# A transformer block on one Trainium2 core: output additions moved at the change of batches, and the last tiles of the down projection begun early

## The chip, the cores and the metric

The kernel runs on one core of a Trainium2 chip. The metric is the device time in microseconds (us) of one execution; lower is better. Engines are named as in the profile: PE is TensorE, DVE VectorE, ACT ScalarE, POOL GpSimd, SP SyncE, which issues all the DMAs here.

## What is computed

```python
mod = (_silu(c) @ wmod).reshape(4, 6, 1, -1)
sa, ca, ga, sb, cb, gb = (mod[:, i] for i in range(6))
...
h = _layernorm(x) * (1 + ca) + sa
x = x + ga * gated_delta_attention(h)
h = _layernorm(x) * (1 + cb) + sb
x = x + gb * ((silu(h @ w_gate.T) * (h @ w_up.T)) @ w_down.T)
```

`x` is (4, 512, 512) in float32, the hidden size of the last line is 2048. The change touches that last line alone, the feed-forward part.

## The kernel before

The first half of the program does the attention part and stores its result `x` to `scrX`. From about 520 us on the feed-forward part runs as 16 iterations (`iteration(it)`, L1011). Iterations 0 to 7 do the batches 0 and 1, iterations 8 to 15 the batches 2 and 3; each iteration does 256 of the 2048 hidden units for 1024 tokens. Every step is written once into a plan (`step(...)`), and each engine goes through the plan and takes the steps that concern it. So the order of the steps in the plan is the order on each engine, and what an engine waits for is written as semaphores.

One iteration has these steps.

- Two products of seven parts, for gate (`n = 2 * it`) and up (`n = 2 * it + 1`): `prod(n, 0..6)` on PE, six matmuls each. Float32 numbers are split into a high and a low part. ACT copies (`copy_s`, three of them for each `n`) and DVE additions (`cadd`) combine the parts; `prod` 2, 4 and 5 wait for one such copy each.
- The weights of the next product: loaded by SP (`w_load`), combined by four operations of POOL (`w_comb`, L2683 to L2689), high part by ACT (`w_high`), low part by seven operations of POOL (`w_low_ff`, L2696). The down weights have ACT and then four POOL operations (`w_high_d`, L2704). `prod(n, 0)` waits for the low part.
- `silu` (ACT), `gated` (DVE), the rounding of the result (`fh`, ACT) and its low part (`fl`, DVE).
- `down(it, k)` for eight tiles `k` of 128 tokens: six matmuls into one of the banks 6 and 7 in turn, then DVE adds the bank to the row `YA[k]` (iterations 0 and 8 copy). PE may write a bank again once DVE has read it. `down(it - 1, k)` stands among the products of iteration `it`.

At the end of iteration 7's sums DVE multiplies each row `YA[k]` by the gate (`post_0`); in iteration 8 POOL adds the stored `x` (`add_0`, L2732, 512 columns, eight operations), and SP stores the eight rows (`store_0`). `down` of iteration 8 writes `YA[k]` anew in iteration 9.

In the last iteration POOL prepares each row with two operations of 512 columns (`out_pre`, L2739 and L2742): `YA[k]` by the gate `gbB`, then plus `XO[k]`, which is the stored `x`. `down(15, k)` then needs two DVE operations: the bank by the gate, and plus `YA[k]` (L2565 on). `XO[0]` to `XO[5]` are loaded in iteration 10; `XO[6]` and `XO[7]` lie where the gate weights are and are loaded in iteration 15:

```python
if 6 in st["ks"]:
    e.wait_ge(sem("prod"), 7 * 30 + 7)
    e.wait_ge(*at_least(w_low_at[45]))
...
for k in st["ks"]:
    e.dma_start(XO[k][:, :], scrX[2 + k // 4, k % 4 * 128:k % 4 * 128 + 128, :]).then_inc(
        sem(f"d_x{2 + k // 4}"), 16)
```

The second operation of `out_pre` waits for `e.wait_ge(sem(f"d_x{2 + k // 4}"), 80 + 64)`. Before these loads the semaphore stands at 80, and each row adds 16, so for `k` from 4 to 7 it takes the rows 4, 5, 6 and 7.

Of the kernel before, what the change touches and what calls it, by code (L numbers as in the profile page):

```python
# [53 lines left out]
def build(nc, x, W1, cw, dtb, alog, nw, Wo, cT, wmod, wgu, wdn, cst, out):  # L54
# [840 lines left out]
    def down(it, k):  # L895
        i, free = ring_bank()
        step("down", it=it, k=k, bank=i, free=free)
        tick("down")
        ring_free[i] = [tick("v_y")]
        if it == 7:  # L900
            step("post_0", k=k)
        if it == 14:
            step("out_pre", k=k)

# [106 lines left out]
    def iteration(it):  # L1011
# [36 lines left out]
        elif it:  # L1048
            prod(n, 0)
            prod(n, 1)  # L1050
            copy_s(n, 0)
            flush()
            prod(n, 2)
            cadd(n, 0)
            prod(n, 3)
            copy_s(n, 1)
            if last:
                w_high(up_m(it), [("prod", 7 * (n - 1) + 7)])
            step("silu", it=it, t=0)
            prod(n, 4)  # L1060
            copy_s(n, 2)
            cadd(n, 1)
            down(it - 1, 0)
            if not last:
                w_high(up_m(it), [("prod", 7 * (n - 1) + 7)])
            step("silu", it=it, t=1)
            w_load_next(it, w_low_ff(up_m(it)))
            prod(n, 5)
            prod(n, 6)
            step("silu", it=it, t=2)  # L1070
            cadd(n, 2)
            step("silu", it=it, t=3)
        if not last:
            w_comb(gate_m(it + 1))
        for k in range(1, 7):
            if it and (it < 15 or k < 4):
                down(it - 1, k)
            if it in (1, 2) and k in (1, 2, 3, 4):
                turn_tile(4 * it - 4 + k - 1)
                if it == 1:  # L1080
                    step("load_xf", n=k + 3)
# [41 lines left out]
        cadd(n, 1)  # L1123
        if it and not last:
            down(it - 1, 7)
        if turn:
            split_h(1, 4, [("prod", 7 * n + 5)])
            w_high_d(7)
        else:
            gated(it, 1)  # L1130
            w_high_d(it)
            if it == 8:
                for k in range(8):
                    step("add_0", k=k)
            fh(it, 1)
# [130 lines left out]
    def sync(e):  # L1266
# [21 lines left out]
        for st in plan:  # L1288
# [152 lines left out]
            elif kind == "store_0":  # L1441
                k = st["k"]
                e.wait_ge(sem("p_out"), k + 1)
                e.dma_start(out[k // 4, k % 4 * 128:k % 4 * 128 + 128, :], X1[k][:, :]).then_inc(sem("d_out"), 16)
            elif kind == "load_xo":
# [9 lines left out]
            elif kind == "down" and st["it"] == 15:  # L1455
                k = st["k"]
# [5 lines left out]
    def tensor(e):  # L1462
# [11 lines left out]
        for st in plan:  # L1474
# [370 lines left out]
            elif kind == "down":  # L1845
# [9 lines left out]
                for jj, t_ in enumerate(((0, 2), (3, 1))[b]):  # L1855
                    f = f_of(it, t_)
                    t = mm3(bank(st["bank"]), FH[f][:, tk], FL[f][:, tk], WDh[it // 15][:, jj, :], WDl[it // 15][:, jj, :], jj == 0, jj == 1)
                t.then_inc(sem("down"), 1)

# [318 lines left out]
    def vector(e):  # L2178
# [16 lines left out]
        for st in plan:  # L2195
# [357 lines left out]
            elif kind == "down":  # L2553
# [3 lines left out]
                if it % 8 == 0:  # L2557
                    if it:
                        e.wait_ge(sem("p_out"), k + 1)
# [4 lines left out]
                elif it < 15:  # L2564
                    e.wait_ge(sem("v_y"), 8 * (it - 1) + k + 1)  # L2565
                    tt(y, bank(st["bank"]), y, ALU.add).then_inc(sem("v_y"), 1)
                else:
                    e.wait_ge(sem("p_out"), 8 + 2 * k + 2)
                    tt(XO[k][:, :], bank(st["bank"]), gbB[k // 4][:, :], ALU.mult).then_inc(sem("v_y"), 1)
                    e.wait_ge(sem("v_y"), 8 * it + k + 1)  # L2570
                    tt(y, y, XO[k][:, :], ALU.add).then_inc(sem("out_x"), 1)
            elif kind == "post_0":
# [6 lines left out]
    def gpsimd(e):  # L2579
# [11 lines left out]
        for st in plan:  # L2591
# [125 lines left out]
            elif kind == "split_h" and st["on"] == "p":  # L2717
# [8 lines left out]
                signal(t, "p_hs")  # L2726
            elif kind == "add_0":
                k = st["k"]
                e.wait_ge(sem("v_om"), k + 1)
                e.wait_ge(sem(f"d_x{k % 2}"), (160, 144)[k % 2])  # L2730
                in_order()
                signal(e.tensor_tensor(X1[k][:, :], YA[k][:, :], X1[k][:, :], ALU.add), "p_out")  # L2732
            elif kind == "out_pre":
                k = st["k"]
                e.wait_ge(sem("v_y"), 112 + k + 1)
                if k == 0:
# [5 lines left out]
                signal(e.tensor_tensor(YA[k][:, :], YA[k][:, :], XO[k][:, :], ALU.add), "p_out")  # L2742

# [74 lines left out]
```

## Time and profile before

| what | value |
|---|---|
| median of three runs | 1050.65 us |
| lowest, highest | 1048.23, 1051.37 us |
| the profiled execution | 1049.25 us |
| its span | 1047.3 us |
| PE, PEld busy | 996.5, 787.9 us |
| DVE, POOL, ACT busy | 688.9, 555.9, 501.2 us |
| mean granted clock of PE | 0.99 |
| DMA | 106.35 MB |

The span is what the profile covers; the execution's own time is 1.95 us longer. A row of the timeline gives the start and the duration of neighbouring instructions of one kind, their number, and in brackets how long the engine had been idle before them and what ended that.

### The profile page before, as it was taken

The page shows a single profiled execution, that of the slowest core. Times are in us where ns is not written, and L with a number is a line of the kernel's source. Part 1 is how long each engine was busy: PE and PEld are TensorE (multiplying, and loading weights), DVE is VectorE, ACT ScalarE, POOL GpSimd, SP SyncE. Part 2 cuts the span into 40 slices and gives each one's busy share as a digit, 9 for nine tenths or more (in the row PEclk, how much of TensorE's full clock was granted, in tenths as well). Part 3 has the DMA queues.
Part 4 walks back from the last instruction along what each step waited for, and adds up shares of the span by engine and source line. Part 5 has one row for each costly group of instructions (what it writes and reads, how often), then busy time and mean ns, then how long its engine had stood idle before and what let it go on. Part 6 is the DMA issues. An engine that isn't in the chain of part 4 may idle for free.

```text
span 1047.3 us, 20631 instructions
## 1 busy us (share of the span) xinstructions
PE 996.5 (95%) x7920; PEld 787.9 (75%) x7920; DVE 688.9 (66%) x1044; ACT 501.2 (48%) x891; POOL 555.9 (53%) x597
## 2 busy tenths in 40 slices
PE   7999999999998999999799999999989899999997
PEld 4676777878677888888577777888867688878875
DVE  5977377899964777877763455555577455555447
ACT  3676575345545444554555644334453244434340
POOL 1222530022025554658566555877788866657675
PEclk9999999999998999999999999999999999999999
DMA  6504336938356566656242111111131232111112
GB/s 217 201 11 123 76 82 166 261 101 207 78 127 172 117 136 143 158 122 150 77 141 81 41 42 60 40 61 44 58 118 61 104 121 61 41 61 41 41 41 80
DMA packets 158209, 106.35 MB, mean 102 GB/s; under 512 B 93984, under 2 KB 131104, under 8 KB 157984
## 3 DMA queue, kind: packets, MB, share of 16 engines
q1 hardware_dynamic: 158112, 105.04, 35.9%
q8 instruction: 63, 1.03, 0.4%
q14 instruction: 34, 0.28, 0.1%
HBM read 75.65 MB, written 29.36 MB: 100 GB/s over the span
## 4 chain that ended last, share of the span: by engine, by line
PE 61%; POOL 11%; DVE 11%; ACT 5%; issue 5%; DMA 4%; SPq 2%; POOLq 0%; DVEq 0%; ACTq 0%
PE ps L1464 58%; ACT t L1862 5%; POOL t L2696 4%; DVE t L2180 3%; PE ps L1472 3%; DVE t L2290 2%; DMA scrU<-t 2%; SPq L1325 1%; POOL t L2732 1%; DVE t L2278 1%; PE ps L1703 1%; POOL t L2704 1%; POOL t L2725 1%; DVE t L2390 1%; DVE t L2190 1%
## 5 line engine op out<-in xcount | busy, mean ns | idle before, releaser
L1464 PE MATMUL ps<-t,t 128*128 128x512 f32 (+7 forms) x7100 | 942.5, 326 | 45.1 <-ACT t L1862 13.3
L1464 PEld LDWEIGHTS ps<-t,t 128*128 128x128 f32 (+4 forms) x7100 | 734.6, 160 | 238.2 <-issue 46.3
L2180 DVE TENSOR_TENSOR t<-ps,t 128x512 f32<-128x512 f32 (+2 forms) x336 | 234.3, 707 | 228.6 <-PE ps L1464 156.0
L1862 ACT ACTIVATE t<-t 128x512 fp32r<-128x512 f32 (+11 forms) x433 | 271.3, 650 | 220.8 <-DVE t L2180 95.5
L1862 ACT ACTIVATE t<-ps 128x512 f32<-128x512 f32 (+5 forms) x250 | 138.2, 560 | 244.0 <-PE ps L1464 226.4
L2180 DVE TENSOR_TENSOR t<-t,t 128x512 fp32r<-128x512 f32 (+15 forms) x249 | 208.8, 859 | 44.3 <-ACT t L1862 34.4
L2696 POOL TENSOR_TENSOR t<-t,t 128x256 fp32r<-128x256 f32 x217 | 160.7, 776 | 100.7 <-ACT t L1862 100.1
L1862 ACT ACTIVATE t<-ps,t 128x64 f32<-128x64 f32 (+3 forms) x157 | 74.3, 534 | 25.5 <-PE ps L1472 12.3
L2290 DVE SCALAR_TENSOR_TENSOR t<-ps,t,t 128x511 f32<-128x511 f32 (+2 forms) x108 | 80.2, 747 | 3.4 <-ACT t L1862 0.5
L2704 POOL TENSOR_TENSOR t<-t,t 128x256 fp32r<-128x256 f32 x64 | 63.6, 1024 | 17.3 <-ACT t L1862 15.9
L2627 POOL MEMSET t<- 128x3072 f32 x4 | 10.7, 2668 | 92.5 <-PE ps L1464 70.0
L1472 PE MATMUL ps<-t,t 128*128 128x128 f32 (+1 forms) x340 | 53.7, 288 | 1.6 <-DVE t L2185 1.3
L2671 POOL TENSOR_TENSOR t<-t,t 128x768 fp32r<-128x768 f32 x16 | 29.3, 1830 | 33.5 <-ACT t L1862 33.3
L1472 PEld LDWEIGHTS ps<-t,t 128*128 128x128 f32 (+1 forms) x340 | 39.0, 148 | 10.6 <-issue 5.4
L2608 POOL TENSOR_TENSOR t<-t,t 128x384 fp32r<-128x384 f32 x16 | 14.6, 915 | 52.6 <-PE ps L1464 32.7
L2597 POOL TENSOR_TENSOR t<-t,t 128x512 fp32r<-128x512 f32 x13 | 17.4, 1338 | 46.9 <-ACT t L1862 45.8
L2677 POOL TENSOR_TENSOR t<-t,t 128x512 f32<-128x512 f32 x16 | 21.4, 1337 | 38.1 <-DVE t L2180 37.4
L2683 POOL TENSOR_TENSOR t<-t 128x256 f32<-128x256 f32 x32 | 27.1, 847 | 4.6
L1862 ACT ACTIVATE t<-t,t 128x1 f32<-128x1 f32 (+2 forms) x36 | 13.2, 367 | 33.5 <-DVE t L2192 30.5
L2687 POOL TENSOR_TENSOR t<-t 128x256 f32<-128x256 f32 x32 | 26.4, 825 | 2.5
L2190 DVE BATCH_NORM_STATS2 t<-t 128x6 f32<-128x512 f32 x32 | 21.9, 684 | 8.1 <-DMA t<-in_x 6.4
L2632 POOL MEMSET t<- 128x1536 f32 x1 | 1.4, 1381 | 47.3 <-PE ps L1464 47.3
(60 smaller groups left out, 405.5 us busy)
## 6 DMA issues: line engine op xcount, KB each, us to landing
t<-in_wgu SPq DMA_DIRECT2D x32, 512.0 KB, 3.5
scrU<-t SPq DMA_DIRECT2D x60, 256.0 KB, 3.1
t<-scrU SPq DMA_DIRECT2D x32, 288.0 KB, 4.7
t<-in_wdn SPq DMA_DIRECT2D x32, 256.0 KB, 2.8
t<-scrU SPq DMA_DIRECT2D x32, 192.0 KB, 3.4
t<-in_W SPq DMA_DIRECT2D x19, 256.0 KB, 2.9
t<-in_x SPq DMA_DIRECT2D x16, 256.0 KB, 4.1
t<-in_wmod SPq DMA_DIRECT2D x4, 1024.0 KB, 5.5
```

Source lines behind the costliest of these rows:

```text
L1464: return e.matmul(o, l, r_, start=start, stop=stop, skip_group_check=True)
L1472: return e.transpose(o, i, idn)
L1862: return e.activation(o, i, f, **kw)
L2180: return e.tensor_tensor(o, a, b, op)
L2190: e.bn_stats(st6[:, slot_, :], src).then_inc(sem(name + "bn"), 1)
L2290: e.scalar_tensor_tensor(yy[:, d + 1:SEQ], p_[:, 0:SEQ - d - 1], cwt[:, j, 2 - d:3 - d], yy[:, d + 1:SEQ], ALU.mult, ALU.add).then_inc(sem ...
L2671: signal(e.tensor_tensor(OZl[:, :, :], OZ[:, :, :], OZh[:, :, :].bitcast(f32), ALU.subtract), "p_ozl")
L2677: signal(e.tensor_tensor(YB[u % 2][:, :], YB[u % 2][:, :], XB[u % 2][:, :], ALU.add), "p_x1")
L2683: signal(e.tensor_tensor(r_[:, 4, :], r_[:, 0, :], r_[:, 3, :], ALU.add), "p_ws")
L2687: signal(e.tensor_tensor(r_[:, 0, :], r_[:, 1, :], r_[:, 0, :], ALU.subtract), "p_ws")
L2696: t = e.tensor_tensor(WGl[m % 3][:, i, :], WR[st["slot"]][:, i, :], WGh[m % 3][:, i, :].bitcast(f32), ALU.subtract)
L2704: t = e.tensor_tensor(WDl[it // 15][:, n, q], WDr[n][:, q], WDh[it // 15][:, n, q].bitcast(f32), ALU.subtract)
```

## The change

At the switch the eight additions `add_0` move from POOL to DVE: rows 0 and 1 behind gate 1 of iteration 8, rows 2 to 4 at its end, rows 5 to 7 in iteration 9 behind `down(8, 1)` to `down(8, 3)`. The stores move to the end of iteration 9. At the end, `down(14, k)` for `k` from 4 to 7 leaves its sum in a bank of its own (`down_begun`, banks 0, 1, 2 and 6), tile 4 ahead of `prod(31, 5)`, and `down_last` of iteration 15 adds to it there; the four DVE sums in between go. Rows 4 and 5 are prepared ahead of the low part of the last up weights, rows 0 to 3 next, rows 6 and 7 last, behind a wait for `fl(15, 3)`. The two operations of `out_pre` become two halves of 256 columns each.

```diff
+    HELD = {4: 0, 5: 1, 6: 2, 7: 6}
+    LAST = {0: (7, lambda: ring_free[7]), 1: (4, lambda: [("v_c", 95)]), 2: (5, lambda: [("v_c", 96)]),
+            3: (3, lambda: [("v_gf", 63)])}
+
+    def down_begun(k):
+        free = ring_free[6] if HELD[k] == 6 else [("v_c", 93), ("a_si", 63)]
+        step("down_begun", k=k, bank=HELD[k], free=free)
+        tick("down")
+
+    def down_last(k):
+        i, free = (HELD[k], lambda: []) if k in HELD else LAST[k]
+        step("down_last", k=k, bank=i, free=free(), begun=k in HELD)
...
             if last:
                 w_high(up_m(it), [("prod", 7 * (n - 1) + 7)])
+                out_pre(4)
+                out_pre(5)
+                w_low_ff(up_m(it))
             step("silu", it=it, t=0)
             prod(n, 4)
             copy_s(n, 2)
             cadd(n, 1)
             down(it - 1, 0)
+            if last:
+                out_pre(0)
...
-            w_load_next(it, w_low_ff(up_m(it)))
+            if not last:
+                w_load_next(it, w_low_ff(up_m(it)))
...
+            if last and k < 4:
+                out_pre(k)
+            if it == 9 and k < 4:
+                add_0(k + 4)
...
-        if it and not last:
+        if last:
+            down_begun(4)
+        elif it:
             down(it - 1, 7)
...
             if it == 8:
-                for k in range(8):
-                    step("add_0", k=k)
+                add_0(0, 1)
             fh(it, 1)
...
         if it == 8:
+            add_0(2, 3, 4)
+        if it == 9:
             for k in range(8):
                 step("store_0", k=k)
...
-    for k in range(4, 8):
-        down(14, k)
+    for k in range(5, 8):
+        down_begun(k)
+    for k in (6, 7):
+        out_pre(k, [("v_fl", 64)])
     for k in range(8):
-        down(15, k)
+        down_last(k)
```

In `down_last` PE waits for `w_low_at[47]`, the low part of the last down weights, ahead of tile 0, and starts a new sum only in tiles 0 to 3. In POOL's `out_pre`:

```diff
-                e.wait_ge(sem("v_y"), 112 + k + 1)
+                e.wait_ge(sem("v_y"), (104 if k > 3 else 112) + k + 1)
...
-                signal(e.tensor_tensor(YA[k][:, :], YA[k][:, :], gbB[k // 4][:, :], ALU.mult), "p_out")
+                for q in (slice(0, 256), slice(256, 512)):
+                    t = e.tensor_tensor(YA[k][:, q], YA[k][:, q], gbB[k // 4][:, q], ALU.mult)
+                signal(t, "p_out")
                 e.wait_ge(sem(f"d_x{2 + k // 4}"), 80 + 64)
```

**The order on VectorE at the switch.** Here `ps` is PSUM, t_244<-t_244,t_266 is `post_0` of row 7, t_216<-t_232,t_216 gate 1 and t_217<-ps,t_217 gate 2 of iteration 8; t_249 to t_256 are the rows `X1[0]` to `X1[7]`, t_237 to t_244 the rows `YA[0]` to `YA[7]`. Before:

```order
L2180 TENSOR_TENSOR t_244<-t_244,t_266 128x512
L2180 TENSOR_TENSOR t_216<-t_232,t_216 128x512
L2180 TENSOR_TENSOR t_217<-ps,t_217 128x512
L2180 TENSOR_TENSOR t_234<-ps,t_211 128x512
L2180 TENSOR_TENSOR t_218<-t_234,t_218 128x512
L2180 TENSOR_TENSOR t_226<-t_216,t_220 128x512
L2180 TENSOR_TENSOR t_227<-t_217,t_221 128x512
L2180 TENSOR_TENSOR t_228<-t_218,t_222 128x512
L2180 TENSOR_TENSOR t_213<-ps,t_210 128x512
```

Now:

```order
L2241 TENSOR_TENSOR t_244<-t_244,t_266 128x512
L2241 TENSOR_TENSOR t_216<-t_232,t_216 128x512
L2241 TENSOR_TENSOR t_249<-t_237,t_249 128x512
L2241 TENSOR_TENSOR t_250<-t_238,t_250 128x512
L2241 TENSOR_TENSOR t_217<-ps,t_217 128x512
L2241 TENSOR_TENSOR t_234<-ps,t_211 128x512
L2241 TENSOR_TENSOR t_218<-t_234,t_218 128x512
L2241 TENSOR_TENSOR t_226<-t_216,t_220 128x512
L2241 TENSOR_TENSOR t_227<-t_217,t_221 128x512
L2241 TENSOR_TENSOR t_251<-t_239,t_251 128x512
L2241 TENSOR_TENSOR t_252<-t_240,t_252 128x512
L2241 TENSOR_TENSOR t_253<-t_241,t_253 128x512
```

Two additions stand between gate 1 and gate 2, three more between the `fl` steps.

**The order on GpSimd in the last iteration.** t_187 is the low part of iteration 14's down weights, t_185 that of the last up weights; t_265 and t_266 are the gates of batches 2 and 3, t_257 to t_264 the rows `XO[0]` to `XO[7]`. Before:

```order
L2704 TENSOR_TENSOR t_187<-t_181,t_186 128x256 x2
L2739 TENSOR_TENSOR t_237<-t_237,t_265 128x512
L2742 TENSOR_TENSOR t_237<-t_237,t_257 128x512
L2696 TENSOR_TENSOR t_185<-t_179,t_183 128x256 x7
L2739 TENSOR_TENSOR t_238<-t_238,t_265 128x512
L2742 TENSOR_TENSOR t_238<-t_238,t_258 128x512
L2739 TENSOR_TENSOR t_239<-t_239,t_265 128x512
L2742 TENSOR_TENSOR t_239<-t_239,t_259 128x512
L2739 TENSOR_TENSOR t_240<-t_240,t_265 128x512
```

Now:

```order
L2772 TENSOR_TENSOR t_187<-t_181,t_186 128x256 x2
L2804 TENSOR_TENSOR t_241<-t_241,t_266 128x256 x2
L2809 TENSOR_TENSOR t_241<-t_241,t_261 128x256 x2
L2804 TENSOR_TENSOR t_242<-t_242,t_266 128x256 x2
L2809 TENSOR_TENSOR t_242<-t_242,t_262 128x256 x2
L2764 TENSOR_TENSOR t_185<-t_179,t_183 128x256 x7
L2804 TENSOR_TENSOR t_237<-t_237,t_265 128x256 x2
L2809 TENSOR_TENSOR t_237<-t_237,t_257 128x256 x2
L2804 TENSOR_TENSOR t_238<-t_238,t_265 128x256 x2
L2809 TENSOR_TENSOR t_238<-t_238,t_258 128x256 x2
```

The rows 4 and 5 (t_241, t_242) have come ahead of the seven operations of t_185, row 0 (t_237) has gone behind them.

## Rows read from the trace of the kernel before

**Rows 1.** The page: the span, and busy time, share and instructions of each engine.

```profile
span 1047.3 us, 20631 instructions
...
PE 996.5 (95%) x7920; PEld 787.9 (75%) x7920; DVE 688.9 (66%) x1044; ACT 501.2 (48%) x891; POOL 555.9 (53%) x597
```

**Rows 2.** Timeline of TensorE: start, duration, operation, count, [idle before <- releaser].

```profile
781.46 8.68 PE L1464 MATMUL ps<-t,t 128*128 128x512 f32 x30 [2.62 <-issue]
...
814.87 11.25 PE L1464 MATMUL ps<-t,t 128*128 128x512 f32 x48 [1.33 <-ACT t L1862]
826.62 3.03 PE L1464 MATMUL ps<-t,t 128*128 128x512 f32 x12 [0.50 <-POOL t L2696]
832.21 34.10 PE L1464 MATMUL ps<-t,t 128*128 128x512 f32 x141 [2.56 <-ACT t L1862]
```

**Rows 3.** Timeline of GpSimd at the switch.

```profile
809.30 1.53 POOL L2732 TENSOR_TENSOR t<-t,t 128x512 f32<-128x512 f32 x1 [0.17 <-POOL t L2704]
...
821.67 4.90 POOL L2696 TENSOR_TENSOR t<-t,t 128x256 fp32r<-128x256 f32 x7
```

**Rows 4.** Timeline of ScalarE at the switch.

```profile
807.14 0.58 ACT L1862 ACTIVATE t<-ps 128x512 f32<-128x512 f32 x1
...
813.70 0.63 ACT L1862 ACTIVATE t<-t 128x512 f32<-128x512 f32 x1 [3.64 <-DVE t L2180]
...
814.72 2.21 ACT L1862 ACTIVATE t<-t 128x1792 fp32r<-128x1792 f32 x2
...
829.98 1.70 ACT L1862 ACTIVATE t<-t 128x1792 fp32r<-128x1792 f32 x1 [10.62 <-POOL t L2689]
...
838.23 0.60 ACT L1862 ACTIVATE t<-ps 128x512 f32<-128x512 f32 x1 [2.53 <-PE ps L1464]
```

**Rows 5.** Timeline of VectorE at the switch and one iteration later.

```profile
803.66 2.31 DVE L2180 TENSOR_TENSOR t<-t,t 128x512 f32<-128x512 f32 x2
...
807.27 5.79 DVE L2180 TENSOR_TENSOR t<-t,t 128x512 f32<-128x512 f32 x4
...
843.23 3.27 DVE L2180 TENSOR_TENSOR t<-t,t 128x512 f32<-128x512 f32 x4
...
854.73 0.69 DVE L2180 TENSOR_TENSOR t<-ps,t 128x512 f32<-128x512 f32 x1 [0.65 <-PE ps L1464]
...
861.55 0.69 DVE L2180 TENSOR_TENSOR t<-ps,t 128x512 f32<-128x512 f32 x1 [0.68 <-PE ps L1464]
```

**Rows 6.** Windows of 2 us: busy us (xcount) by engine, clock, DMA share, GB/s.

```profile
782.00:784.00 2.00, 2.00 (x6) 1.51 (x6) 0.81 (x1) 2.00 (x4) 1.32 (x2) 0.50 1.05 396
...
832.00:834.00 2.00, 1.79 (x6) 1.42 (x7) 1.42 (x2) 0.16 (x1) 2.00 (x3) 0.74 0.00 0
...
1012.00:1014.00 2.00, 1.49 (x6) 1.24 (x7) 0.00 (x0) 0.00 (x0) 1.75 (x2) 1.00 0.03 8
```

**Rows 7.** Timeline of TensorE at the end.

```profile
1012.51 7.10 PE L1464 MATMUL ps<-t,t 128*128 128x512 f32 x30 [1.71 <-POOL t L2696]
1020.29 5.78 PE L1464 MATMUL ps<-t,t 128*128 128x512 f32 x24 [0.69 <-ACT t L1862]
1027.86 15.30 PE L1464 MATMUL ps<-t,t 128*128 128x512 f32 x60 [1.79 <-DVE t L2180]
```

**Rows 8.** Timeline of GpSimd at the end.

```profile
1004.72 1.29 POOL L2739 TENSOR_TENSOR t<-t,t 128x512 f32<-128x512 f32 x1 [6.59 <-DVE t L2180]
1006.16 1.29 POOL L2742 TENSOR_TENSOR t<-t,t 128x512 f32<-128x512 f32 x1
1007.60 4.86 POOL L2696 TENSOR_TENSOR t<-t,t 128x256 fp32r<-128x256 f32 x7
```

**Rows 9.** Tile scrX from 1005 to 1012 us: issues, landing.

```profile
L1453 SPq DMA_DIRECT2D t<-scrX x2: 327/380/433, 1006.7 to 1007.1; - x2
...
DMA to landing us min/median/max: 2.7/2.8/2.9
```

**Rows 10.** Timeline of VectorE at the end.

```profile
1039.78 1.05 DVE L2180 TENSOR_TENSOR t<-t,t 128x512 f32<-128x512 f32 x1
```

More of the change, by code:

```diff
@@ L901, in down, with out_pre, out_at, add_0 @@
             step("post_0", k=k)
-        if it == 14:
-            step("out_pre", k=k)
+    out_order = []
+    def out_pre(k, free=()):
+        step("out_pre", k=k, free=list(free))
+        out_order.append(k)
+    def out_at(k):
+        return 2 * out_order.index(k) + 2
+    def add_0(*ks):
+        for k in ks:
+            step("add_0", k=k)
+    HELD = {4: 0, 5: 1, 6: 2, 7: 6}
[8 more added lines that the diff above has]
+        step("down_last", k=k, bank=i, free=free(), begun=k in HELD)
+        tick("down")
+        tick("v_y")
     def gate_row(b):
@@ L1442, in sync @@
                 k = st["k"]
-                e.wait_ge(sem("p_out"), k + 1)
+                e.wait_ge(sem("v_om"), 8 + k + 1)
                 e.dma_start(out[k // 4, k % 4 * 128:k % 4 * 128 + 128, :], X1[k][:, :]).then_inc(sem("d_out"), 16)
@@ L1454, in sync @@
                         sem(f"d_x{2 + k // 4}"), 16)
-            elif kind == "down" and st["it"] == 15:
+            elif kind == "down_last":
                 k = st["k"]
@@ L1857, in tensor @@
                     t = mm3(bank(st["bank"]), FH[f][:, tk], FL[f][:, tk], WDh[it // 15][:, jj, :], WDl[it // 15][:, jj, :], jj == 0, jj == 1)
+                t.then_inc(sem("down"), 1)
+            elif kind in ("down_begun", "down_last"):
+                k = st["k"]
+                b, s = k // 4, k % 4
+                tk = slice(s * 128, (s + 1) * 128)
+                ahead = kind == "down_begun"
+                it = 14 if ahead else 15
+                for tok in st["free"]:
+                    e.wait_ge(*at_least(tok))
+                if ahead and k == 4:
+                    e.wait_ge(sem("v_fl"), 60)
+                elif not ahead and s == 0:
+                    e.wait_ge(sem("v_fl"), 64 if b else 63)
+                if not ahead and k == 0:
+                    e.wait_ge(*at_least(w_low_at[47]))
+                opens = ahead or not st["begun"]
+                for jj, t_ in enumerate(((0, 2), (3, 1))[b]):
+                    f = f_of(it, t_)
+                    t = mm3(bank(st["bank"]), FH[f][:, tk], FL[f][:, tk], WDh[it // 15][:, jj, :], WDl[it // 15][:, jj, :],
+                            opens and jj == 0, not ahead and jj == 1)
                 t.then_inc(sem("down"), 1)
@@ L2558, in vector @@
                     if it:
-                        e.wait_ge(sem("p_out"), k + 1)
+                        e.wait_ge(sem("v_om"), 8 + k + 1)
                     else:
@@ L2563, in vector @@
                     e.tensor_copy(y, bank(st["bank"])).then_inc(sem("v_y"), 1)
-                elif it < 15:
+                else:
                     e.wait_ge(sem("v_y"), 8 * (it - 1) + k + 1)
                     tt(y, bank(st["bank"]), y, ALU.add).then_inc(sem("v_y"), 1)
[L2567 to L2571, printed above, removed]
+            elif kind == "down_last":
+                k = st["k"]
+                e.wait_ge(sem("down"), 120 + k + 1)
+                e.wait_ge(sem("p_out"), out_at(k))
+                tt(XO[k][:, :], bank(st["bank"]), gbB[k // 4][:, :], ALU.mult).then_inc(sem("v_y"), 1)
+                e.wait_ge(sem("v_y"), 116 + k + 1)
+                tt(YA[k][:, :], YA[k][:, :], XO[k][:, :], ALU.add).then_inc(sem("out_x"), 1)
+            elif kind == "add_0":
+                k = st["k"]
+                e.wait_ge(sem("v_om"), k + 1)
+                e.wait_ge(sem(f"d_x{k % 2}"), (160, 144)[k % 2])
+                tt(X1[k][:, :], YA[k][:, :], X1[k][:, :], ALU.add).then_inc(sem("v_om"), 1)
             elif kind == "post_0":
@@ L2726, in gpsimd @@
                 signal(t, "p_hs")
[L2727 to L2732, printed above, removed]
             elif kind == "out_pre":
                 k = st["k"]
-                e.wait_ge(sem("v_y"), 112 + k + 1)
-                if k == 0:
+                e.wait_ge(sem("v_y"), (104 if k > 3 else 112) + k + 1)
+                for tok in st["free"]:
+                    e.wait_ge(*at_least(tok))
+                if k == 4:
                     e.wait_ge(sem("a_grow"), 6)
                 in_order()
-                signal(e.tensor_tensor(YA[k][:, :], YA[k][:, :], gbB[k // 4][:, :], ALU.mult), "p_out")
+                for q in (slice(0, 256), slice(256, 512)):
+                    t = e.tensor_tensor(YA[k][:, q], YA[k][:, q], gbB[k // 4][:, q], ALU.mult)
+                signal(t, "p_out")
                 e.wait_ge(sem(f"d_x{2 + k // 4}"), 80 + 64)
                 in_order()
-                signal(e.tensor_tensor(YA[k][:, :], YA[k][:, :], XO[k][:, :], ALU.add), "p_out")
+                for q in (slice(0, 256), slice(256, 512)):
+                    t = e.tensor_tensor(YA[k][:, q], YA[k][:, q], XO[k][:, q], ALU.add)
+                signal(t, "p_out")
     final = {"proj": n_proj, "merge_b": 16, "a_cout": count["a_cout"], "a_mg": count["a_mg"], "v_mg": count["v_mg"]}
```

## The prediction

> **What bounds the kernel now.** I read the page first: TensorE is busy for 996.5 of 1047.3 us [rows 1], so a step pays only where TensorE stands still. The profiled execution took 1049.25 us, 1.95 more than its span. The timeline of TensorE then gives its pauses at the two places that the change touches.
>
> At the switch (iterations 8 and 9) TensorE pauses 1.33, 0.50 and 2.56 us [rows 2]. GpSimd shows why: eight additions of 512 columns start at 809.30, and only at 821.67 does it split the up weights of iteration 9, which TensorE takes at 826.62 [rows 3, 2]. The next combinations then make ScalarE wait until 829.98, and the copy behind them is what TensorE waits for until 832.21 [rows 4, 2]. The pause of 1.33 has another cause: four VectorE operations take 5.79 us beside these additions, against 3.27 one iteration later [rows 5], and ScalarE waits 3.64 us for them [rows 4]. The windows show one more cost: TensorE's granted clock, else 1.00 (2.4 GHz), is 0.74 on average from 832 to 834, so part of that stretch ran at 0.50, 1.2 GHz [rows 6]. Six matmuls, one product or one tile of `down`, take 1.365 us at the full clock (six tiles from 854.73 to 861.55, five distances [rows 5]). ScalarE's copy behind the third product after the restart at 832.21 was due 4.1 us later, at 836.3, and comes at 838.23 [rows 4]: the fall costs 1.9 us. A pause of 2.62 at 781.46 was also followed by a fall (0.50 at 782); one of 1.71 at 1012.51 was not [rows 2, 6, 7].
>
> At the end TensorE pauses 1.71 for GpSimd's split of the last up weights, 0.69 for a copy, 1.79 for VectorE [rows 7]. Its last 60 matmuls take 15.30 us instead of the 13.65 of their usual pace, since it waits for VectorE to empty two banks in turn.
>
> **The switch, part by part.** The eight additions leave GpSimd: it is free from 809.13 and splits the up weights at once when ScalarE has made their high part (it is in the 2.21 us of two activations from 814.72 [rows 4]). The waits of 0.50 and 2.56 us are gone. They come back as VectorE work: two between the gates 1 and 2 of iteration 8, three behind, three in iteration 9 between the copies of `down`.
>
> The first two matter. VectorE finishes the multiplication before at 805.97 [rows 5], GpSimd is in `w_high_d` until 809.13 [rows 3], and beside such 256-column work two operations took 2.31 us [rows 5]. So the two additions cost 2.0 to 2.3 us, bounded below by 1.2 (two of 0.6, their pace when GpSimd rests) and above by 2.9 (1.45 each, as in the 5.79). Behind them wait gate 2, ScalarE's rounding of it, and behind that in ScalarE's order the first copy of iteration 9, done at 807.72 now [rows 4]. TensorE takes its third product right behind that copy; at six matmuls per 1.365 us it could have begun at 807.33. So a new pause of 2.4 to 2.7 us opens there, 2.0 to 2.3 of it new. The five VectorE operations after gate 2 and the three added ones put the silu and the copy behind it near 816.0, against 814.87 [rows 2]; the pause of 1.33 shrinks to some 0.4. TensorE is thus 1.1 us late there. The three additions in iteration 9 lie in gaps like the 0.67 us ahead of such a tile's sum [rows 5] and take up to 1.15: with two banks, 0.3 to 0.8 us more. Then the removed 0.50 and 2.56 count: 1.1 + 0.5 − 3.06 = **−1.5 us** (ends −2.6 and −0.7).
>
> *Clock.* The pause of 2.56 that led to the fall is gone (−1.9), but the new one, 2.4 to 2.7, is just as long as the 2.56 and 2.62 that led to one. As it falls on both sides of them I count half: **−0.95 us** (ends −1.9 and 0). The stores move one iteration; SyncE has nothing due there, and their wait costs nothing: the loads behind them are read 150 us later.
>
> **The end, part by part.** The preparation of rows 4 and 5 is put ahead of the split of the last up weights. Its multiplication can start when GpSimd is free, 6.59 us ahead of 1004.72 [rows 8]. But its addition waits for a semaphore at 144, that is for all four rows of batch 3, and rows 6 and 7 are loaded only when iteration 15's gate products are through: issued at 1006.7 and 1007.1, landing up to 2.9 us later, at 1010.0 [rows 9]. In the kernel before nothing urgent waits for them. Now GpSimd stands, and the split of the weights stands behind it in order.
>
> From 1010.0: one addition and two more steps of two halves. Seven 256-column operations take 4.86 us [rows 8], 0.69 each; I take 1.42 for two, and 0.15 lies between two steps (from 1004.72 + 1.29 to 1006.16) [rows 8]: 1.42 + 2 × 1.57 = 4.6, then 0.1 and the split's 4.86. TensorE restarts at 1019.6 instead of 1012.51 (+7.1), after 8.8 us of rest.
>
> What comes back: the begun sum of tile 4 lies over the copy (0.69); tiles 5 to 7 have banks of their own and wait for no VectorE sum (1.79); the last eight tiles too (15.30 − 13.65 = 1.65), all in all: 114 matmuls at 1.365 per six are 25.9, with 0.3 for the last one's end 26.2, so TensorE ends at 1045.85 against 1043.16 [rows 7]: **+2.7 us**. The four sums that VectorE no longer makes there are in this.
>
> *Clock.* A rest of 8.8 us is three times those that led to a fall: **+1.9 us** by the one at 832 (ends 1.7 and 3.0, since after a longer rest it may stay low longer).
>
> *VectorE's last rows.* GpSimd's rows 6 and 7 wait for the last split of iteration 15, near 1037.7, and run to 1044 or 1045, beside VectorE's first four or five tiles. Its additions take 1.05 beside such rows now [rows 10], against 0.69 alone; a pair is then 1.7 us against TensorE's 1.365, and a lag builds that 1.33 per pair later hardly recovers: **+0.9 us** (ends 0 and 1.4). The low part of the last down weights comes at 1035 to 1037, where TensorE asks for it at 1036.6: 0 to 0.8, counted at nothing, hidden by the products of iteration 15. Sum of the end: **+5.5 us** (ends +4.4 and +7.9).
>
> **Halving.** Two halves take 1.42 where one operation takes 1.29 [rows 8]; 0.13 each, three of them ahead of the split: 0.4 us, in the sum. In return VectorE waits for shorter operations. The Trainium skill (SBUF — State Buffer, "SBUF: two separate sides") says that an operation of VectorE with two SBUF inputs and one of GpSimd exclude each other for a whole instruction. By that rule each of the two first additions could wait a full 0.73 and take 1.33, 2.7 for both instead of 2.0 to 2.3, and the sum would be 0.4 worse; the trace's 1.15 per operation, averaged, stays below it and is what I use.
>
> **Sum.** −1.5 − 0.95 + 5.5 = +3.05 us. On the profiled execution that is 1052.3; the median of the three runs, 1050.65, lies 1.4 above that execution, so the forecast for a median is **1053.7 us**, 0.29% slower. A measurement of this kernel tells about 0.3%, 3.15 us, from no change, so this lies on the border of slower and same.
>
> **Rivals.**
> 1. *The load is not in the way* (faster). If rows 6 and 7 were there before GpSimd asks, the preparation of rows 4 and 5 would fit into GpSimd's idle 6.59 us ahead of 1004.72 [rows 8]: 4 × 1.57 = 6.3 from 998.2, the split from 1004.5 to 1009.4, no pause at 1010.8. TensorE would end at 1010.8 + 26.2 = 1037.0, 6.2 earlier; with 0.9 of VectorE's lag −5.3, and −2.45 at the switch: 1049.25 − 7.75 = 1041.5, or 1042.9 for a median. For it: the order of the steps has room for it there. Against it: the wait value and the issue at 1006.7 in the trace. It decides if the landing is before 1003. Chance 0.07.
> 2. *Clock low at both places and longer* (clearly slower). The two additions take 1.45 each, the new pause is over 2.62 and the clock falls there (+0.95); after 8.8 us it stays low for 3.0 us' worth (+1.1); VectorE's lag is 1.4 (+0.5): +5.6, 1054.9, or 1056.3 for a median. For it: each end has its row. It decides from a pause of 2.6 us on at 807. Chance 0.33.
> 3. *The switch gains in full* (same). The two additions fall between GpSimd's operations at 0.6 to 0.9 each, the pause at 807 stays under 2 us, as the 1.71 that led to no fall: −2.6 − 1.9 + 5.5 = +1.0, 1050.25, or 1051.7 for a median. Chance 0.25.
>
> The forecast keeps 0.35. It lies half on each side of 0.3%; rival 2 is slower, rival 3 within: slower 0.175 + 0.30 = 0.48 (a little of rival 2 stays within), same 0.45, faster 0.07. The range leaves out rival 1 and the far ends: 1049.5 to 1057.5.
>
> **What would show it.** Right: a pause of TensorE of 8 to 9 us ahead of its restart near 1018 (all times 1.5 to 3 earlier at this point by the gain at the switch), GpSimd idle for some 10 us between the two steps of row 4, the clock at 0.50 behind it; a pause of 2 to 3 us at the third product of iteration 9, and none at 826 to 832. Wrong: GpSimd's addition of row 4 directly behind its multiplication, or no pause near 807.

## The result, and the profile after

| kernel | median | lowest, highest | runs |
|---|---|---|---|
| before | 1049.18 us | 1046.99, 1051.37 us | 8 |
| changed | 1053.09 us | 1050.22, 1057.57 us | 8 |

The ratio is 1.0043, with a 95% interval from 1.0029 to 1.0057: slower by 0.4%. The interval leaves out no change, though its lower end, 0.29%, is just under the 0.3% that the prediction took as what a measurement can't tell from no change. The forecast was 1053.7, on a base of 1050.65. The profiled execution took 1051.8 us, its span is 1049.8 us, and TensorE's mean granted clock is 0.986.

The busy times on the profile's page are within 5 us of those before: neither the gain nor the loss shows there.

```profile
span 1049.8 us, 20640 instructions
...
PE 994.9 (95%) x7920; PEld 788.4 (75%) x7920; DVE 690.5 (66%) x1048; ACT 501.4 (48%) x891; POOL 551.6 (53%) x605
```

The timeline of TensorE answers to [rows 2] and [rows 7]. Its columns are start, duration, line, operation, count, and in brackets the idle time before and its releaser.

```profile
796.76 11.25 PE L1505 MATMUL ps<-t,t 128*128 128x512 f32 x48 [0.45 <-ACT t L1923]
810.45 49.75 PE L1505 MATMUL ps<-t,t 128*128 128x512 f32 x216 [2.44 <-ACT t L1923]
...
1015.51 17.80 PE L1505 MATMUL ps<-t,t 128*128 128x512 f32 x66 [8.79 <-POOL t L2764]
1033.60 11.33 PE L1505 MATMUL ps<-t,t 128*128 128x512 f32 x48 [0.29 <-DVE t L2241]
```

At the switch the three pauses of 1.33, 0.50 and 2.56 us have become one of 2.44, at the third product of iteration 9. At the end the pauses of 1.71, 0.69 and 1.79 have become one of 8.79 and one of 0.29.

VectorE at the switch, against [rows 5]: the group of four is the last `post_0`, gate 1 and the two additions, and the first two of these took 2.31 before.

```profile
803.99 4.66 DVE L2241 TENSOR_TENSOR t<-t,t 128x512 f32<-128x512 f32 x4
808.57 1.27 DVE L2241 TENSOR_TENSOR t<-ps,t 128x512 f32<-128x512 f32 x2
```

ScalarE behind it, against [rows 4]: the rounding of gate 2 waits 2.29 us for VectorE, and the copy at 809.82, behind which TensorE goes on at 810.45, stands behind that rounding.

```profile
809.28 0.63 ACT L1923 ACTIVATE t<-t 128x512 fp32r<-128x512 f32 x1 [2.29 <-DVE t L2241]
809.82 0.58 ACT L1923 ACTIVATE t<-ps 128x512 f32<-128x512 f32 x1
```

GpSimd at the end, against [rows 8]. L2804 is the multiplication of `out_pre`, L2809 the addition; L2764 is the split of the last up weights.

```profile
994.22 2.13 POOL L2804 TENSOR_TENSOR t<-t,t 128x256 f32<-128x256 f32 x2 [0.17 <-POOL t L2772]
1006.00 1.42 POOL L2809 TENSOR_TENSOR t<-t,t 128x256 f32<-128x256 f32 x2 [9.65 <-DMA t<-scrX]
1007.56 1.40 POOL L2804 TENSOR_TENSOR t<-t,t 128x256 f32<-128x256 f32 x2
1009.11 1.40 POOL L2809 TENSOR_TENSOR t<-t,t 128x256 f32<-128x256 f32 x2
1010.65 4.80 POOL L2764 TENSOR_TENSOR t<-t,t 128x256 fp32r<-128x256 f32 x7
```

The view of the tile `scrX` from 1000 to 1012 us, against [rows 9], names the waiter, where the same view of the kernel before has none:

```profile
L1494 SPq DMA_DIRECT2D t<-scrX x2: 327/380/432, 1002.6 to 1003.0; - x2
...
  POOL t L2809: 9.6, 1
...
DMA to landing us min/median/max: 2.7/2.8/2.9
```

1003.0 + 2.9 is 1005.9, and GpSimd's addition starts at 1006.00. TensorE restarts when the seven operations of the split are through.

The windows (busy time and count of PE, PEld, DVE, ACT and POOL; then clock, DMA share, GB/s) show the clock, against [rows 6]. At the switch it stays at 1.00, that is 2.4 GHz; in the long rest it falls to 0.50 before TensorE has restarted, and comes back between 1020 and 1022.

```profile
812.00:814.00 2.00, 2.00 (x11) 1.65 (x10) 2.00 (x4) 0.60 (x1) 0.00 (x0) 1.00 0.31 120
...
1010.00:1012.00 2.00, 0.00 (x0) 0.00 (x0) 0.00 (x0) 0.00 (x0) 1.86 (x3) 0.61 0.00 0
...
1016.00:1018.00 2.00, 2.00 (x6) 1.52 (x6) 0.00 (x0) 0.00 (x0) 1.86 (x4) 0.50 0.03 8
...
1020.00:1022.00 2.00, 2.00 (x9) 1.63 (x8) 0.89 (x2) 0.00 (x0) 1.71 (x4) 0.83 0.00 0
```

**Where the time went.** ScalarE's copy behind the first product of iteration 15 is a point that both kernels have. It starts at 997.12 us before and at 993.04 us now:

```profile
997.12 0.60 ACT L1862 ACTIVATE t<-ps 128x512 f32<-128x512 f32 x1 [0.86 <-PE ps L1464]
```

```profile
993.04 0.60 ACT L1923 ACTIVATE t<-ps 128x512 f32<-128x512 f32 x1 [0.87 <-PE ps L1505]
```

From the run of matmuls at 796 on (796.41 before, 796.76 now) that is 200.71 against 196.28: the switch gave 4.4 us. From this copy on, TensorE's restart comes after 15.39 us before and 22.47 now (+7.1), its end after 46.04 and 51.89 (+5.85), and the end of VectorE's last operation after 47.7 and 54.36 (+6.7). Against the 4.4 and a start 0.35 later this makes the 2.5 us between the two spans, to 0.1. The medians lie 3.9 apart: one profile is one execution, and in the experiments below the switch alone gave less than 4.4 in the median.

### The profile page after: what moved, and what is told of

The parts are those of the page before. It is cut to its first block, busy times and chain, and to the rows that moved or that the text cites. A ratio compares the mean times of both kernels' runs of the same rounds, so it can differ in the third digit from the quotient of the medians.

```text
span 1049.8 us, 20640 instructions
## 1 busy us (share of the span) xinstructions
PE 994.9 (95%) x7920; PEld 788.4 (75%) x7920; DVE 690.5 (66%) x1048; ACT 501.4 (48%) x891; POOL 551.6 (53%) x605
## 4 chain that ended last, share of the span: by engine, by line
PE 66%; DVE 10%; POOL 8%; ACT 5%; issue 5%; DMA 3%; SPq 3%; DVEq 0%; POOLq 0%; ACTq 0%
PE ps L1505 62%; ACT t L1923 5%; DVE t L2241 3%; PE ps L1513 3%; POOL t L2764 3%; DVE t L2351 2%; DVE t L2339 1%; DMA scrU<-t 1%; PE ps L1744 1%; SPq L1366 1%; POOL t L2793 1%; DVE t L2251 1%; DVE t L2451 1%; SPq L1426 1%; DMA t<-scrA 1%
## 5 line engine op out<-in xcount | busy, mean ns | idle before, releaser
L2241 DVE TENSOR_TENSOR t<-ps,t 128x512 f32<-128x512 f32 (+2 forms) x332 | 231.2, 707 | 232.0 <-PE ps L1505 168.4
L2241 DVE TENSOR_TENSOR t<-t,t 128x512 fp32r<-128x512 f32 (+14 forms) x257 | 214.3, 855 | 44.0 <-ACT t L1923 33.8
L2764 POOL TENSOR_TENSOR t<-t,t 128x256 fp32r<-128x256 f32 x217 | 161.2, 779 | 105.8 <-ACT t L1923 105.3
L2751 POOL TENSOR_TENSOR t<-t 128x256 f32<-128x256 f32 x32 | 27.6, 862 | 4.6
L2755 POOL TENSOR_TENSOR t<-t 128x256 f32<-128x256 f32 x32 | 26.4, 825 | 2.5
L2757 POOL TENSOR_TENSOR t<-t 128x256 f32<-128x256 f32 x32 | 25.1, 785 | 2.5
```

Source lines behind the costliest of these rows:

```text
L2241: return e.tensor_tensor(o, a, b, op)
L2751: signal(e.tensor_tensor(r_[:, 4, :], r_[:, 0, :], r_[:, 3, :], ALU.add), "p_ws")
L2755: signal(e.tensor_tensor(r_[:, 0, :], r_[:, 1, :], r_[:, 0, :], ALU.subtract), "p_ws")
L2757: signal(e.tensor_tensor(r_[:, 6, :], r_[:, 2, :], r_[:, 5, :], ALU.subtract), "p_ws")
L2764: t = e.tensor_tensor(WGl[m % 3][:, i, :], WR[st["slot"]][:, i, :], WGh[m % 3][:, i, :].bitcast(f32), ALU.subtract)
```

## The experiments

Each kernel was timed against the kernel before on the same chip; a ratio is to that. The kernel before had medians of 1049.18 us beside the change, 1048.54 beside the first four experiments below, 1049.32 beside the next four and 1049.15 beside the last two. So a difference of medians between kernels of different groups carries up to 0.8 us that are not the kernels'.

**The switch alone.** The kernel before, with the eight additions on VectorE and the stores in iteration 9 as in the change, and the end as before.

```diff
+            if it == 9 and k < 4:
+                add_0(k + 4)
...
-                for k in range(8):
-                    step("add_0", k=k)
+                add_0(0, 1)
...
         if it == 8:
+            add_0(2, 3, 4)
+        if it == 9:
```

> The kernel before with the switch of the change alone (additions on VectorE, stores one iteration later). Theory from the two profiles (the copy behind the first product of iteration 15 comes 4.4 us earlier from one start): 2.5 to 4.5 us less than the kernel before; 4.4 where the clock does not fall at the new pause near 808 us, 2.5 where it does. My prediction had 2.45. Rival: the added VectorE work gives it back, 0 to 1 us.

Measured: 1046.24 us (12 runs), ratio 0.9976, from 0.9961 to 0.9992. Its profile has the same pause, and this time the clock fell behind it:

```profile
810.99 39.40 PE L1471 MATMUL ps<-t,t 128*128 128x512 f32 x164 [2.44 <-ACT t L1869]
```

```profile
810.00:812.00 2.00, 1.01 (x3) 0.82 (x4) 1.90 (x4) 1.56 (x3) 0.46 (x1) 0.86 0.26 55
812.00:814.00 2.00, 2.00 (x6) 1.56 (x5) 2.00 (x4) 0.43 (x1) 0.00 (x0) 0.50 0.55 207
```

So the switch is a gain, 2.3 us by the medians, a little under the 2.5 to 4.5 expected; the rival's 0 to 1 is only at the far end of the interval (0.8 to 4.1). The 4.4 us of the profile of the change are an execution without this fall; what the fall costs is worked out below.

**The end alone.** The change with the eight additions back on GpSimd in iteration 8, and the stores there.

```diff
-            if it == 9 and k < 4:
-                add_0(k + 4)
...
-                add_0(0, 1)
+                add_0(*range(8))
...
-            add_0(2, 3, 4)
-        if it == 9:
```

> The kernel before with the end of the change alone (additions stay on GpSimd). Theory: the end alone costs 6 to 7 us (a restart 7.1 us later, 2.6 of clock, some 0.8 of VectorE, less the pauses that go), so 1055 to 1057. If the two parts add up, e2 and e3 against the kernel before sum to the change's own difference of 3.9. Rival: the two parts meet (GpSimd or the clock carries one into the other), and the sum misses that by over 2 us.

Measured: 1055.63 us (6 runs), ratio 1.0066, from 1.0042 to 1.0090: 7.1 us slower by the medians. −0.24% and +0.66% make +0.42%, where the change has +0.43%. By the medians −2.3 and +7.1 make 4.8 us against 3.9, still within the 2 us of its rival. The parts add up as far as these runs can tell, and the end is the whole loss. TensorE's pause is the same as in the change:

```profile
1020.60 17.45 PE L1501 MATMUL ps<-t,t 128*128 128x512 f32 x66 [8.78 <-POOL t L2755]
```

**Only the own load waited for.** The loads of rows 6 and 7 count on another semaphore, so that rows 4 and 5 wait for their own loads alone, made in iteration 10.

```diff
-                        sem(f"d_x{2 + k // 4}"), 16)
+                        sem(f"d_x{2 + k // 4}" if k < 6 else "d_wo"), 16)
...
-                e.wait_ge(sem(f"d_x{2 + k // 4}"), 80 + 64)
+                e.wait_ge(*((sem("d_wo"), 48) if k > 5 else (sem(f"d_x{2 + k // 4}"), 80 + (32 if k > 3 else 64))))
```

> The change with one difference: rows 6 and 7 of the stored x are counted on a semaphore of their own, so rows 4 and 5 no longer wait for them. Theory (the load is what stops GpSimd): the wait of 9.65 us of GpSimd is gone, TensorE has no pause of 8.8 us and no low clock at the end; it should end 7.1 + 2.6 us earlier than in the change less what other waits appear, so some 8 to 10 us less than the change, 1043 to 1045 us, and faster than the kernel before by 5 to 7. Rival (the place of the two preparations on GpSimd is what costs, whatever they wait for): a pause of about 6 us before the last up product stays, and the time stays within 2 us of the change.

Measured: 1043.67 us (12 runs), ratio 0.9954, from 0.9938 to 0.9971: 9.4 us below the change by the medians, as the theory had it. GpSimd's addition of row 4 follows its multiplication, and the split is through at 1004.1:

```profile
991.87 2.13 POOL L2804 TENSOR_TENSOR t<-t,t 128x256 f32<-128x256 f32 x2 [0.17 <-POOL t L2772]
994.14 1.71 POOL L2809 TENSOR_TENSOR t<-t,t 128x256 f32<-128x256 f32 x2
...
999.15 4.92 POOL L2764 TENSOR_TENSOR t<-t,t 128x256 fp32r<-128x256 f32 x7
...
1018.86 3.48 POOL L2772 TENSOR_TENSOR t<-t,t 128x256 fp32r<-128x256 f32 x4
```

The long pause is gone, and a new one has come, for the last row of these: the split of the last down weights stands behind the preparation of rows 0 to 3, ahead of `down_last(0)`.

```profile
1022.49 12.75 PE L1505 MATMUL ps<-t,t 128*128 128x512 f32 x48 [2.98 <-POOL t L2772]
```

The window from 1022 to 1024 has the clock at 0.55 on average, the next one at 0.59; the expectation had no low clock at the end.

**The early rows moved behind the weights.** The change with rows 4 and 5 prepared behind the split of the last up weights instead of ahead of it; the shared semaphore stays.

```diff
+                w_low_ff(up_m(it))
                 out_pre(4)
                 out_pre(5)
-                w_low_ff(up_m(it))
```

> The change with the preparation of rows 4 and 5 put behind the low part of the last up weights; the load and its wait stay. Theory: no pause before the last up product, but GpSimd still waits for the load (to 1006) and then has six preparations of 3.1 us and the down weights, so TensorE waits 3 to 5 us for the low part of the last down weights ahead of the last eight tiles, with or without a fall of the clock: 1046 to 1050, 3 to 7 less than the change. Rival (the pause is made by the weights being late for another reason): the pause ahead of the last up product stays above 5 us.

Measured: 1049.03 us (12 runs; the ratio is without one of 4488.49 us), ratio 0.9998, from 0.9978 to 1.0018. The wait for the load has shrunk to 1.44 us, and no up weights stand behind it. But all of GpSimd's preparation is now between the up and the down weights, and TensorE waits 6.79 us for those, where 3 to 5 were expected:

```profile
1005.74 1.44 POOL L2809 TENSOR_TENSOR t<-t,t 128x256 f32<-128x256 f32 x2 [1.44 <-DMA t<-scrX]
...
1025.48 2.76 POOL L2772 TENSOR_TENSOR t<-t,t 128x256 fp32r<-128x256 f32 x4
```

```profile
1028.39 14.00 PE L1505 MATMUL ps<-t,t 128*128 128x512 f32 x48 [6.79 <-POOL t L2772]
```

Of the 9.4 us that the own semaphore gives, this gives 4.1. Here the end hangs on GpSimd's order: its twelve steps between the up and the down weights, 1.6 to 2.3 us each with the gap behind it, are more than the products of iteration 15 hide.

**The additions on VectorE spread.** The change, with no more than two additions in a row: one at the end of iteration 8, two behind the first `cadd` of iteration 9, two behind its first `down`, three as in the change. None stands between gate 1 and gate 2.

```diff
             cadd(n, 0)
+            if it == 9:
+                add_0(1, 2)
...
             down(it - 1, 0)
+            if it == 9:
+                add_0(3, 4)
...
-                add_0(0, 1)
+                pass
...
-            add_0(2, 3, 4)
+            add_0(0)
```

> The change with its eight VectorE additions spread otherwise: none between the gates 1 and 2, one at the end of iteration 8, two behind the first cadd of iteration 9, two behind down(8, 0), three as in the change. Theory (the two additions hold back gate 2, the rounding and the copy): the pause of 2.44 us near 808 is gone; the first copy of iteration 9 is 2.3 us earlier; 2 to 3 us less than the change, more where the change's own pause had let the clock fall. Rival: the pause only moves to the copy behind the silu, as 1.3 us in the kernel before, and the gain is under 1 us.

Measured: 1049.99 us (12 runs), ratio 1.0005, from 0.9992 to 1.0019: 3.1 us below the change by the medians, 0.38% by the ratios. TensorE has no pause at the switch, and the one at the end is as long as before:

```profile
796.33 53.84 PE L1509 MATMUL ps<-t,t 128*128 128x512 f32 x231 [0.45 <-ACT t L1927]
...
1012.96 17.66 PE L1509 MATMUL ps<-t,t 128*128 128x512 f32 x66 [8.73 <-POOL t L2768]
```

So the 2.44 us were the price of where these additions stood, and could be had back. This edit moves five of them; that the two ahead of gate 2 made the pause follows from the order on VectorE, as in the forecast, and no run moved these two alone.

**Not halved.** The change with both operations of `out_pre` on 512 columns, as before.

```diff
-                for q in (slice(0, 256), slice(256, 512)):
-                    t = e.tensor_tensor(YA[k][:, q], YA[k][:, q], gbB[k // 4][:, q], ALU.mult)
-                signal(t, "p_out")
+                signal(e.tensor_tensor(YA[k][:, :], YA[k][:, :], gbB[k // 4][:, :], ALU.mult), "p_out")
...
```

> The change with the operations that prepare the output rows whole again, 512 columns. Theory: 0.13 us less for each of the three steps ahead of the last up weights and as much for each later one; TensorE restarts 0.4 us earlier, the low part of the last down weights comes 1.5 us earlier, VectorE's last additions wait a little longer each: 0.4 to 1 us less than the change, which is within the spread. Rival (halving is what keeps VectorE's last rows short): 1 us or more above the change.

Measured: 1051.23 us (12 runs), ratio 1.0025, from 1.0008 to 1.0042, against 1.0043 (1.0029 to 1.0057) in halves. The intervals overlap. The profile shows what there is: each step at the pace of the first line below, against 1.40 to 1.42 in halves, and a pause of 8.44 us where it was 8.79. Behind the pause the 114 matmuls to the end took 28.09 us, where the change has 29.42 (17.80, 0.29 and 11.33): the clock was back sooner, its average 0.74 in the window from 1016 to 1018 and 1.00 from there on. So the clock makes more of the difference between these two profiles than the halving does.

```profile
1006.50 1.26 POOL L2803 TENSOR_TENSOR t<-t,t 128x512 f32<-128x512 f32 x1
```

```profile
1014.16 28.09 PE L1505 MATMUL ps<-t,t 128*128 128x512 f32 x114 [8.44 <-POOL t L2764]
```

**Own load, not halved.** Both edits together.

> e1 (own semaphore for rows 6 and 7) with whole operations. In e1 a pause of 2.98 us remained, behind GpSimd's low part of the last down weights, and a fall of the clock behind it. Theory (GpSimd's time bounds the end there, and halves cost 0.13 us a step): ten steps ahead of that low part make it 1.3 to 1.8 us earlier, the pause 1.2 to 1.7, without or with a rarer fall of the clock: 1.5 to 3 us less than e1. Rival: no difference to e1 beyond 0.5.

Measured: 1042.47 us (6 runs), ratio 0.9941, from 0.9920 to 0.9961; 1.2 us below the halves by the medians, under the 1.5 to 3 expected, and again with overlapping intervals: the times don't settle it, the profile says more. GpSimd comes to the last down weights 23.9 us after its first multiplication of row 4, where in halves it took 27.0 (991.87 to 1018.86):

```profile
995.87 1.53 POOL L2803 TENSOR_TENSOR t<-t,t 128x512 f32<-128x512 f32 x1 [0.17 <-POOL t L2772]
...
1019.75 3.73 POOL L2772 TENSOR_TENSOR t<-t,t 128x256 fp32r<-128x256 f32 x4
```

These 3.1 us of twelve steps are the pause of 2.98, which is gone. Undisturbed, a step takes 1.43 us in halves and 1.29 whole, which makes 1.7 of the 3.1. The other 1.4 come from the six steps in each kernel that took longer, 1.71 to 2.20 in halves and 1.53 to 1.57 whole; what held them is not shown.

```profile
1024.13 11.30 PE L1505 MATMUL ps<-t,t 128*128 128x512 f32 x48 [0.40 <-DVE t L2241]
```

**Own load, and row 3 behind the last down weights.** In halves.

```diff
-            if last and k < 4:
+            if last and k < 3:
                 out_pre(k)
...
             w_high_d(it)
+            if last:
+                out_pre(3)
```

> e1 with the preparation of row 3 put behind the low part of the last down weights, halves kept. Theory: the low part is there 3 us earlier, 0.5 us before TensorE asks; the pause of 2.98 and the fall of the clock are gone: 3 to 4.5 us less than e1, 1039 to 1041. Rival: VectorE or the last rows on GpSimd then set the end, and the gain is under 1.5.

Measured: 1041.57 us (6 runs), ratio 0.9926, from 0.9904 to 0.9947. It is 2.1 us below own load in halves by the medians, where 3 to 4.5 and 1039 to 1041 us were expected: a miss, and the intervals overlap. TensorE runs through the end without a pause:

```profile
994.76 40.64 PE L1507 MATMUL ps<-t,t 128*128 128x512 f32 x176
```

In this execution the clock fell to 0.50 behind the pause at the switch, as it did in the one with own load and whole operations, and not in the one with own load in halves. So the profiles show the gain of the end best by itself: from the copy behind the first product of iteration 15 to the end of VectorE's last operation it takes 47.7 us in the kernel before, 46.3 with own load, 43.4 with own load and whole operations and 43.2 here, that is 3.1 less than with own load alone.

**All of it, in halves.** Own load, row 3 behind, and the additions spread.

> The change in halves, with three edits together: the loads of output rows 4 and 5 waited for by themselves, the preparation of row 3 behind the last iteration's down weights, and VectorE's eight additions at the switch spread (1 at the end of iteration 8, 2 behind the first combining copy of iteration 9, 2 behind its first down product, 3 as before). If the pause of 2.41 to 2.44 us at the switch is what the four additions in a row cost, and the clock that falls behind it in some executions is theirs too, this is 2 to 3.5 us below the same kernel without the spread: 1038 to 1039.5, ratio 0.989 to 0.991. Rival: the additions in the new places hold up VectorE's gate products or evictions there, and it comes out at 1041 to 1043, no better than before the spread.

Measured: 1038.65 us (5 runs), ratio 0.9894, from 0.9874 to 0.9914: 1.1% faster than the kernel before. The timeline of TensorE is one row from the switch to the end:

```profile
796.78 234.24 PE L1511 MATMUL ps<-t,t 128*128 128x512 f32 x1012 [0.46 <-ACT t L1929]
```

It is 2.9 us below the kernel ahead by the medians and 0.32% by the ratios, about what the spread gave in the change; the two intervals overlap slightly, and the two were timed on different chips. The rival, VectorE late elsewhere, did not come.

**All of it, not halved.**

> As the kernel beside it, with GpSimd's preparing operations on 512 columns. If halving costs only through the time GpSimd takes (0.13 to 0.15 us per step, some 8 steps of the end off TensorE's path now), this is within 1 us of the halves: 1037.5 to 1039.5. If long single operations keep VectorE waiting at the end or at the switch, it is 1 us or more above the halves.

Measured: 1039.0 us (4 runs), ratio 0.9895, from 0.9875 to 0.9914. The two medians are 0.35 us apart: once no wait of TensorE hangs on GpSimd's preparation, halves and whole operations can't be told apart. (This profile has one pause of TensorE near the end, 0.95 us at 1020.33, for which it shows no releaser.)

## Why the prediction was right, point by point

**The number** came out 0.6 us from the forecast, and that is in part luck. The forecast stood on a median of three runs, 1050.65, and eight runs gave 1049.18, 1.5 less; the difference to the kernel before was forecast at +3.05 us (0.29%) and measured at +3.9 (0.43%, from 0.29% to 0.57%), 0.9 more. The two errors work against each other. So do two in the parts: the end cost more than forecast, and in the profile the switch gave more.

**The end's mechanism** held in each step. The wait for all four rows of batch 3, the landing as the end of that wait, the split behind it in GpSimd's order: GpSimd sat 9.65 us, TensorE restarted 7.1 us later than before (forecast 7.1) after a pause of 8.79 (forecast 8.8). The own semaphore shows it to be the cause: that one edit took the wait and the long pause away, and 9.4 us with them.

**TensorE behind the restart** was 5.85 us late at its end, where the forecast had 4.6 (2.7 and 1.9 for the clock). From the restart on it took 29.42 us instead of the 26.2 of the forecast. The term that was too small is the clock, "+1.9 us by the one at 832": the 66 matmuls behind the restart took 17.80 us, and as many took 15.34 in the kernel before, at a clock of 1.00:

```profile
758.92 15.34 PE L1464 MATMUL ps<-t,t 128*128 128x512 f32 x66 [0.26 <-ACT t L1862]
```

The clock cost 2.5, inside the ends of 1.7 and 3.0 that the forecast gave. That the other pauses go was right but for 0.29.

**VectorE's lag** grew from 1.66 us (1044.82 − 1043.16) to 2.47 (1047.40 − 1044.93): +0.8, forecast +0.9. The additions beside GpSimd's last rows took 1.08 and twice 1.21, 1.4 us over the 0.69 of three undisturbed ones; later pairs make up for a part of it:

```profile
1038.33 0.68 DVE L2241 TENSOR_TENSOR t<-ps,t 128x512 f32<-128x512 f32 x1
1039.05 1.21 DVE L2241 TENSOR_TENSOR t<-t,t 128x512 f32<-128x512 f32 x1
...
1046.71 0.69 DVE L2241 TENSOR_TENSOR t<-t,t 128x512 f32<-128x512 f32 x1
```

In all the end is +6.7 in the profile and +7.1 by the medians of the end alone (its interval is +4.4 to +9.4), against +5.5 forecast, within its ends of 4.4 and 7.9.

**The switch** was forecast at −2.45 and measured at −2.3 in the median of the switch alone, whose interval, −0.8 to −4.1, tells little of so near a match. Its parts were less exact. The new pause at the third product is there with 2.44 us (2.4 to 2.7). The two additions took 4.66 − 2.31 = 2.35 us, a little over the 2.0 to 2.3. The Trainium skill (SBUF — State Buffer, "SBUF: two separate sides") has the two engines exclude each other for a whole instruction. By that rule 2.7 was the most; the 2.35 stays below it, and no run here puts the rule to a test. The remaining pause of "some 0.4" at 815 did not open, nor did the 0.3 to 0.8 for the banks in iteration 9.

The profiles settle what the waits and the clock are worth, by the stretch from the run of matmuls near 796 to the copy behind the first product of iteration 15:

| profile | run starts | copy | between | clock behind the pauses |
|---|---|---|---|---|
| before | 796.41 | 997.12 | 200.71 | fell at 832 |
| the end alone | 799.00 | 998.13 | 199.13 | did not fall |
| the switch alone | 797.29 | 995.12 | 197.83 | fell at 811 |
| the change | 796.76 | 993.04 | 196.28 | did not fall |
| the additions spread | 796.33 | 990.54 | 194.21 | no pause |

The other kernels repeat the last three rows: 196.3 us in three without a fall, 197.8 in two with one, 194.2 in the two best. So the fall costs 1.5 to 1.6 us of such a stretch, not 1.9; with the clock the same in both, the switch gives 2.9 (199.13 − 196.28), where the step "1.1 + 0.5 − 3.06" had 1.5; and the spread gives 2.1 more. That step was too cautious by 1.4. The median's −2.3 is less than this 2.9, as it would be if the clock fell behind the new pause at least as often as behind the old ones; how often it falls in the runs without a profile isn't shown. So it is by luck that −2.3 is so near −2.45: a gain of the waits that was put too low, and a half fall of the clock that the median doesn't show.

**The halving** was forecast at +0.4 us ahead of the split. The pause became 0.35 shorter without it; by the medians whole operations are 1.9 us faster, which these intervals don't tell from 0.4.

**The rivals.** The first, the load not in the way, did not happen; made by hand it gave 1043.67, where its working had 1042.9. That working missed the pause of 2.98 for the last down weights, counted at nothing because "hidden by the products of iteration 15": with GpSimd's steps earlier, but TensorE earlier still, they weren't. The second, clock low at both places and longer, is right that the clock is low for longer at the end (2.5 us, where it had 3.0), and at the switch in some executions; its 1056.3 took both falls in one execution, and left out the 0.6 to 0.9 us that its two longer additions would themselves have cost. The third's short pause at 807 did not happen.

## What to carry to other kernels

Before a step is put ahead of urgent work on an engine that takes its steps in order, read what its semaphore value really counts: one that is shared by several loads makes the first row wait for the last load, and everything queued behind it too. When such a wait is taken away, look for the next weights or tile that stand behind the same steps, and order the steps by when each is asked for. In this kernel, additions moved to a busier engine made no pause of TensorE where they stood in the gaps of its waits, and one of about their full length between two operations of a chain that feeds TensorE, so spread such work.

## What was not expected of the hardware

The length of a pause did not tell whether the granted clock falls. The pause of 2.41 or 2.44 us at the third product of iteration 9 was followed by a clock of 0.50 in three profiled executions (the switch alone; own load, not halved; row 3 behind) and by none in four (the change, own load, the early rows moved behind, not halved). The pause of 2.56 at 832 led to a fall before [rows 6], and the same one in the end alone, 2.55, did not. A pause of 1.79 at the end led to none in the kernel before and to one in the switch alone:

```profile
1025.88 16.35 PE L1471 MATMUL ps<-t,t 128*128 128x512 f32 x60 [1.79 <-DVE t L2187]
```

```profile
1026.00:1028.00 2.00, 2.00 (x6) 1.62 (x7) 0.42 (x1) 0.00 (x0) 1.86 (x2) 0.62 0.00 0
```

The moment may count more than the length. TensorE has a pause of 2.61 to 2.63 us near 782 in all twelve profiles. The clock fell behind it in the eight whose restart lies between 779.42 and 781.83 us, and not in the four between 781.92 and 784.06 (the switch alone, the end alone, own load not halved, row 3 behind). At the switch it fell behind the three restarts from 810.56 to 811.27, and not behind the four from 808.04 to 810.45. These three are executions without a fall near 782, and the four had one there. No run moved a pause by itself, so this is not shown to be the cause. But an execution without a fall at the switch had paid for one near 782, ahead of the stretch that the table above measures.

Where it did fall at the switch, the clock was low in parts of three windows of 2 us. Behind the rests of 6.8 to 8.8 us it was low for some 3 to 6 us of work: about 3 behind 8.44 (not halved), 5 behind 8.79 (the change), 6 behind 6.79 (the early rows behind). What decides about a pause of about 2 us stays open; a forecast of one is best made with a chance, and where the clock does fall, removing the pause is worth more than its length.
